# Self-edges taken out of layers 1 and 2 of a three-layer graph network: an edge list squeezed by VectorE during layer 0, and 197 steps a layer instead of 208

## What is computed

```python
h = x @ enc_W + enc_b
for l in range(3):
    cat = concatenate([h[src], h[dst], edge_features])            # 64 + 64 + 16
    m = relu(cat @ msg_W1[l] + msg_b1[l]) @ msg_W2[l] + msg_b2[l]
    agg = segment_sum(m, dst)
    h = gru_cell(agg, h, ...)
y = relu(h @ ro_W1 + ro_b1) @ ro_W2 + ro_b2
out = layernorm(x + y)
```

## Time and profile before

| | |
|---|---|
| timed runs, median of 3 | 6154.56 us |
| profiled execution: its own time (span) | 9775.6 us |
| gathers in it | 4830, of 0.955 us mean (4767 of them) |
| busy: GpSimd / VectorE / TensorE / ScalarE | 4639.2 / 3532.6 / 2880.1 / 346.4 us |
| TensorE granted clock | 0.571 mean |

### The profile page before, as it was taken

The page is one execution under the profiler, slowest core; times in us unless marked ns, Lnnn a source line. Parts: engine busy times, 40 slices in busy tenths (PEclk is TensorE's granted clock), DMA queues, the critical chain, the costliest instruction groups (busy, mean ns, idle before and its releaser), DMA issues.

```text
span 9775.6 us, 72182 instructions
## 1 busy us (share of the span) xinstructions
PE 2880.1 (29%) x7290; PEld 1610.2 (16%) x7290; DVE 3532.6 (36%) x4656; ACT 346.4 (4%) x542; POOL 4639.2 (47%) x4865
## 2 busy tenths in 40 slices
PE   3323322322322332222222222223232222322223
PEld 2111111111111221111111111112111111111112
DVE  2333333333333433333333333333333334333334
ACT  0000000000000000000000000000000000000001
POOL 5444444444444454444444444445454445545543
PEclk6555555555555555555555555555555555555555
DMA  3111111111111111111111111111111111111111
GB/s 87 31 31 30 30 30 30 28 31 30 31 30 30 30 28 30 30 30 30 30 30 29 30 30 27 30 31 30 30 31 31 30 30 34 31 31 31 31 30 25
DMA packets 351443, 308.63 MB, mean 32 GB/s; under 512 B 149364, under 2 KB 237518, under 8 KB 350568
## 3 DMA queue, kind: packets, MB, share of 16 engines
q0 software_dynamic: 155328, 159.79, 8.6%
q1 hardware_dynamic: 118271, 110.17, 4.0%
q10 hardware_dynamic: 77328, 33.96, 1.4%
HBM read 280.52 MB, written 22.83 MB: 31 GB/s over the span
## 4 chain that ended last, share of the span: by engine, by line
SPq 57%; issue 38%; DVE 2%; PE 1%; another core or an unknown queue 1%; DMA 0%; ACT 0%; POOL 0%; DVEq 0%; ACTq 0%; POOLq 0%
SPq L473 46%; SPq L469 6%; SPq L642 2%; SPq L633 1%; SPq L527 1%; DVE work_ps L1493 1%; SPq L630 1%; DVE folds L1528 0%; DVE p_src L1490 0%; PE bank L838 0%; DMA p_src<-p_tab 0%; PE work_ps L949 0%; PE bank L962 0%; SPq L662 0%
## 5 line engine op out<-in xcount | busy, mean ns | idle before, releaser
L798 POOL DMA_INDIRECT p_src<-p_tab,idx_all x4767 | 4551.1, 955 | 4916.8 <-DVE work_ps L1493 3467.4
L962 PE MATMUL bank<-hot,folds 128*128 128x96 f32 x2496 | 660.1, 413 | 4012.9 <-issue 2053.0
L1490 DVE TENSOR_TENSOR p_src<-work_ps,p_src 128x512 f32<-128x512 f32 x624 | 427.6, 685 | 3374.9 <-DMA p_src<-p_tab 2912.1
L962 PEld LDWEIGHTS bank<-hot,folds 128*128 128x128 f32 x2496 | 532.1, 296 | 4278.5 <-issue 2198.0
L949 PE MATMUL work_ps<-w_edges,msg 128*128 128x512 f32 x1248 | 1120.0, 997 | 21.4 <-DMA windows_sb<-q_tab 21.4
L1523 DVE SCALAR_TENSOR_TENSOR work_ps<-work_ps,rel 128x1024 f32<-128x1024 f32 x624 | 768.8, 1232 | 21.5
L1493 DVE TENSOR_TENSOR work_ps<-p_src,bank 128x1024 f32<-128x1024 f32 x624 | 767.0, 1229 | 21.4
L1528 DVE TENSOR_REDUCE folds<-work_ps 128x256 f32<-128x1024 f32 x624 | 758.4, 1215 | 0.0
L959 PE MATMUL bank<-hot,counts 128*34 128x96 bf16 x416 | 68.9, 261 | 2248.6 <-issue 1278.6
L1538 DVE TENSOR_TENSOR sums<-bank,sums 128x96 f32 x624 | 158.1, 253 | 872.6 <-remote 699.5
L959 PEld LDWEIGHTS bank<-hot,counts 128*34 128x34 bf16 x416 | 27.1, 108 | 2368.2 <-issue 1359.8
(11 more groups left out here) (167 smaller groups left out, 1800.9 us busy)
## 6 DMA issues: line engine op xcount, KB each, us to landing
p_src<-p_tab ACTq DMA_DIRECT2D x9792, 0.2 KB
p_src<-p_tab SPq DMA_DIRECT2D x9792, 0.2 KB
p_src<-p_tab,idx_all POOLq DMA_INDIRECT x4830
msg<-in_edge_k SPq DMA_DIRECT2D x156, 256.0 KB
pick<-rel_tab SPq DMA_DIRECT2D x312, 96.0 KB
windows_sb<-q_tab ACTq DMA_DIRECT2D x312, 24.0 KB
windows_sb<-q_tab SPq DMA_DIRECT2D x312, 24.0 KB
pick<-q_tab ACTq DMA_DIRECT2D x312, 24.0 KB
```

The costliest lines, as they stand in the source:

```text
L798: pool.indirect_dma_start(out=p_src[r][0:rows, t, :], out_offset=None, in_=p_tab[l][0:NODES, :], in_offset=bass.IndirectOffsetOnAxis(ap=id ...
L962: last = nc.tensor.matmul(fold_ps, folds[:, b, :], hot_all[n % 2][:, s * BLOCKS + b, 1:WINDOW + 1], start=(b == 0), stop=(b == BLOCKS - 1))
L1490: nc.vector.tensor_tensor(rows, edge_ps[k % 2], rows, ALU.add).then_inc(with_edge, 1)
```

## The change

Layer 0 is computed as before, over the whole list. Beside it the kernel makes a second edge list without the self-edges, and layers 1 and 2 use it: 197 steps (`PACKS`), each made from 1,080 edges of the original list, of which at most 1,024 are left. Group inputs of these layers come from tables in HBM that the kernel writes itself (`pack_edges`, `pack_rel_tab`, `pack_src`). The message of the self-edges (now one sum per node) is added per chunk. The parts:

- **Gathers.** `gathers_of`: a layer before has 208 x 8 - 51 - 3 = 1,610. Layers 1 and 2 now have 197 x 8 - 48 = 1,528 each. Layer 0 keeps 1,610.
- **Squeezing** (`press_step`, in groups 1 to 44 of layer 0). Two batches (100 and 97 packs, one pack per partition). Per batch 16 steps of preparation (`prepare`), then 18 planes (positions, sources, 16 edge features), a group each: 7 predicated copies over up to 1,095 elements (`shift`) and one reordering copy. SyncE loads and stores a plane each group.
- **Back into SBUF.** 8 pieces of up to 25 packs (`piece_load`): four transfers each, 128 x 25 runs of 4 words; `make_masks` makes new masks.
- **Loops.** In layer 0 `select_loops` (four VectorE instructions a group, one more input for SyncE), two small matmuls a step and one more add in `keep` give each node the features of its self-edges. In layers 1 and 2 each chunk has a matmul, an activation and an add more, and one ScalarE copy less.
- **Start.** New checks of the list (some 30 VectorE instructions over up to 2,160 elements); TensorE's two matmuls for the ranges stand behind the encoder, where they stood within it.

In the diff, in order: constants, `gathers_of`, SyncE in group g of layer 0, `piece_load`, VectorE's squeezing and `select_loops`, VectorE in a chunk of layers 1 and 2, and the start of TensorE's program.

```diff
+PACK = 1080
+PACK_SINGLES = 48
+BATCHES = ((0, 100), (100, PACKS - 100))
+PREP_GROUPS = 4
+PASS_LOW = (0, 0, 0, 0, 170, 368, 814)
+STEPS_OF = (STEPS, PACKS, PACKS)
...
+        def gathers_of(l, m):
+            return LAST_TILES if l == 0 and m == STEPS - 1 else EDGE_TILES - has_singles(l, m)
...
+                            if batch is not None and at >= PREP_GROUPS:
+                                pack_store(batch, at)
+                            batch, at = job(g - 1)
+                            if batch is not None and (at > PREP_GROUPS or (batch, at) == (1, 0)):
+                                pack_load(batch, at)
+                        for q in range(PIECES_ALL):
+                            if piece_loaded_at(q) == (l, g):
+                                piece_load(q)
...
+            def piece_load(q):
+                first, end = packs_of(q)
+                sp.wait_ge(packed_whole, 16 * (2 if end <= BATCHES[0][1] else 4))
+                sp.wait_ge(joined, end)
...
+                for b in range(BLOCKS):
+                    half = slice(b * RUN, (b + 1) * RUN)
+                    sp.dma_start(idx_all[:, first:end, half].bitcast(I32),
+                                 pack_src[first:end, b * RUN * 128:(b + 1) * RUN * 128].rearrange("u (r g) -> r u g", g=RUN)).then_inc(pack_idx_in, 16)
...
+            def shift(what, k, count):
+                low, high, by = PASS_LOW[k], PASS_HIGH[k], 1 << k
+                squeeze(nc.vector.copy_predicated(what[0:count, low:high], moves[k][0:count], what[0:count, low + by:high + by]))
...
+            def press_plane(batch, at, part):
...
+                if part < 2:
+                    shift(what, 2 * part, count)
+                    shift(what, 2 * part + 1, count)
+                elif part == 2:
+                    for k in range(4, SHIFTS):
+                        shift(what, k, count)
...
+            def select_loops(n):
...
+                nc.vector.tensor_tensor(edge_major[n % 2], edge_major[n % 2],
+                                        loop_runs[:].unsqueeze(2).to_broadcast([128, GROUP * BLOCKS, EDGE_DIM, RUN]), ALU.mult).then_inc(loop_steps, 1)
+                dve.wait_ge(loop_steps, 2 * n + 2)
+                nc.vector.tensor_reduce(loop_sel[n % 2], edge_major[n % 2], AX.X, ALU.add).then_inc(looped, 1)
...
+                if j == 0 and l:
+                    dve.wait_ge(loop_act, nth_loop(l, c) + 1)
+                    dve.wait_ge(kept, last_of(l, c) + 1)
+                    nc.vector.tensor_tensor(chunk_sum[0:HID, 0:w], zr[0:HID, 0:w], sums[0:HID, at + 1:at + 1 + w], ALU.add).then_inc(loop_added, 1)
...
-                if u == RANGES_AFTER:
...
-                    pe.wait_ge(apart_done, 1)
...
+            pe.wait_ge(vw_sb, LAYERS)
+            pe.wait_ge(reduced, 1)
...
+            pe.wait_ge(apart_done, 1)
```

More of the change, by code:

```diff
@@ L449, in nth_late, with where, group_of, begun @@
             return ((l - 1) * EARLY + m) * LATE_HOTS + q * LATE_BLOCKS + b
+        def where(k):
+            l = sum(k >= first for first in FIRST_STEP[1:])
+            return l, k - FIRST_STEP[l]
+        def group_of(l, m):
+            return FIRST_GROUP[l] + m // GROUP
+        def begun(n):
+            l = sum(n >= first for first in FIRST_GROUP[1:])
+            return FIRST_STEP[l] + min(GROUP * (n - FIRST_GROUP[l]), STEPS_OF[l])
+        def job(group):
+            batch, at = divmod(group - FIRST_JOB, BATCH_GROUPS)
+            return (batch, at) if 0 <= batch < len(BATCHES) else (None, None)
@@ L749, in _ @@
             for m in range(PRE):
-                for t in range(gathers_of(m)):
+                for t in range(gathers_of(0, m)):
                     pool.indirect_dma_start(
@@ L795, in _ @@
                             all_stored(pool, l, FAST_CHUNKS)
-                        for t in range(gathers_of(m)):
-                            rows = LAST_ROWS if m == STEPS - 1 and t == LAST_TILES - 1 else 128
+                        for t in range(gathers_of(l, m)):
+                            rows = LAST_ROWS if l == 0 and m == STEPS - 1 and t == LAST_TILES - 1 else 128
                             pool.indirect_dma_start(
@@ new lines, in _ @@
+            measured_by(last)
+            for i, (_, bound) in enumerate(MOST + LEAST):
+                last = nc.vector.tensor_scalar(measured[:, :, i], measured[:, :, i], float(bound), None, ALU.is_gt if i < len(MOST) else ALU.is_lt)
+            measured_by(last)
+            measured_by(nc.vector.tensor_reduce(pair_flags[0:PAIRED, 4:5], measured.rearrange("p j i -> p (j i)"), AX.X, ALU.add))
+            measured_by(nc.vector.tensor_scalar(far[:], row_f[:], 2.0 * PACK_RATE, -PACK_SLACK, ALU.mult, ALU.add))
@@ new lines, in _ @@
+            measured_by(nc.vector.tensor_scalar(pair_flags[:, 1:2], pair_flags[:, 1:2], 0.0, None, ALU.is_lt))
+            for j in range(2):
+                measured_by(nc.vector.tensor_tensor(apart[0:PAIRED], apart[0:PAIRED], measured[:, j, 0:1], ALU.add))
+            measured_by(nc.vector.tensor_tensor(apart[0:1], apart[0:1], measured[0:1, 0, 1:2], ALU.add))
+            measured_by(nc.vector.tensor_reduce(near[:], pair_flags[:], AX.X, ALU.add))
+            nc.vector.tensor_tensor(apart[:], apart[:], near[:], ALU.add).then_inc(apart_done, 1)
@@ new lines, in press_step, with make_masks @@
+            def press_step(m):
+                batch, at = job(m // GROUP)
+                if batch is None:
+                    return
+                if at < PREP_GROUPS:
+                    prepare(batch, at * GROUP + m % GROUP)
+                else:
+                    press_plane(batch, at, m % GROUP)
+            def make_masks(q):
+                first, end = packs_of(q)
+                count = (end - first) * BLOCKS
+                runs = pieces_i[q % 2][:, 0:end - first].rearrange("p u (b g) -> p (u b) g", g=RUN)
+                here = slice(first * BLOCKS, end * BLOCKS)
+                lead_edge = runs[:, :, 0:1].to_broadcast([128, count, RUN])
+                dve.wait_ge(piece_in[q % 2], 16 * BLOCKS * (q // 2 + 1))
+                nc.vector.tensor_copy(rel_first[:].rearrange("p u b -> p (u b)")[:, here], runs[:, :, 0])
+                nc.vector.tensor_tensor(masks[:, here, 0, :], runs, lead_edge, ALU.is_equal)
+                nc.vector.scalar_tensor_tensor(masks[:, here, 1, :], runs, -1.0, lead_edge, ALU.add, ALU.is_equal).then_inc(remasked, 1)
+                dve.wait_ge(remasked, q + 1)
@@ L1473, in landed @@
             def landed(k):
-                return 16 * sum(gathers_of(j % STEPS) for j in range(k % ROW_SLOTS, k + 1, ROW_SLOTS) if j >= PRE)
+                return 16 * sum(gathers_of(*where(j)) for j in range(k % ROW_SLOTS, k + 1, ROW_SLOTS) if j >= PRE)
             def edge_sums(k):
```

549 lines of the change are left out of this document (454 added, 95 removed).

## The result

| | us | beside the kernel before |
|---|---|---|
| before | 6155.32 (6151.95 to 6156.73, 4 runs) | |
| forecast | 6040 (5965 to 6210) | faster |
| after | 6451.16 (6447.2 to 6460.33, 4 runs) | 1.0483, 95% interval 1.0469 to 1.0498: slower |
| after, 100 rows in batch 2 (a run below) | 6087.86 (6085.66 to 6088.72, 4 runs) | 0.9891, interval 0.9874 to 0.9907: 1.1% shorter, clear of noise, but the same by a margin of 2% |

The account below looks back on a forecast made before the run. The prediction took GpSimd's gathers, 1.25 us each, as the bound: 6154.6 - 205 (gathers removed) + 80 (gathers held up by VectorE) + 8 (start) = 6,038, say 6040 us, with VectorE's and SyncE's added work at 0; range 5,965 to 6,210.

Parts of the forecast that it names:

- What bounds the kernel: Timed kernel: GpSimd gathers nearly all the time, 4,830 gathers at 1.25 us each; profiled execution bound by SyncE's single rows.
- Removed, -205 us: Layers 1 and 2: 164 fewer gathers at 1.25 us each, -205 us.
- Added: SyncE in layer 0 ... 0, hidden by that slack: SyncE's queue, layer 0: three more transfers a group, 1.4 us, cost 0 because SyncE has slack.
- slack: SyncE in layer 0: a group's rows, address loads and transfers take 25 us of 39.
- pieces of the list: Loads back into SBUF, seven in layer 0: 22 to 42 us each, cost 0, up to 40 us each without slack.
- VectorE's time, 0: Layer 0: VectorE's added work makes 8.6 us a step, 9.3 of 9.7 with waits, hidden by gathers: 0.
- Rival 2: Predicated copies take two passes an element, 2.3 us each, so VectorE becomes the bound: 6,177 us, chance 0.10.
- Gathers held up, +80 us: Gathers wait for VectorE's port: planes' copies 55 us, preparation 16, loops 5, chunks 4; +80 us, bounds 25 and 350.
- Rivals 1 and 3: 1: predicated copies don't hold gathers, 5,983 us, chance 0.14. 3: port held through whole gathers too, 6,307 us, chance 0.06.
- Start, +8 us: Range matmuls follow the encoder, so GpSimd restarts some 2 us after 95.1 and first step comes later: +8 us, 2 to 20.
- Rival 4: SyncE has no slack if a row takes 0.46 us, not 0.26: +230 us, 6,268 us, chance 0.13; decides from about 0.39.
- profile after: Profile of the changed kernel: again a span set by SyncE, near 9,550 us, with 4,666 gathers.

Follow-up runs that it names:

- rows100_3: The changed kernel with the second batch's loads, stores and squeezing over 100 rows instead of 97: 6087.86 us, 0.9891 of the kernel before.
- short100_2: rows100_3's kernel with the planes' predicated copies cut to 16 elements, lists of layers 1 and 2 not squeezed: 6083.13 us, 0.9885 of the kernel before.
- few100: Changed kernel, 100 rows in second batch, 28 of 64 single rows a group on each of SyncE and ScalarE, other 36 by plain transfers: 6086.16 us, 0.989.
- load100_4: The changed kernel with the second batch's loads of 100 rows and stores still of 97: 6333.55 us, 1.0289 of the kernel before.

## Why the forecast was wrong, step by step

- **What bounds the kernel: right, as far as it can be worked out.** The gathers of layers 1 and 2 follow each other without a wait in rows100_3 (9.77 us a step). 4,830 x 1.26, with 42.6 us ahead of the first gather and 30 behind the last (as in rows100_3), are 6,158 against 6,155 measured: the kernel before has next to no time besides gathers. The sum leaves out the 13.6 us that GpSimd idles before 95.1 us, and 1.26 us is good to some 0.3%, so it is exact to 10 or 20 us, and no trace of the kernel before from the timed kind confirms it. 1.26 us is a better figure than my 1.25, which left 60 us for other things. What I said of the profiled execution was off: it ran at its chip's own pace, and all timings of the kernel before on chips of that kind are as long.
- **Removed, -205 us: right.** 164 x 1.26 = 207; layers 1 and 2 run at 9.8 us a step even with 97 rows in the second batch, against 9.7 forecast.
- **"Added: SyncE in layer 0 ... 0, hidden by that slack": this step failed, by 363 us.** I counted what it takes to issue three more transfers (1.4 us) and never asked how long a plane's store and load themselves take, nor that an issue can wait behind them. Both transfers were in the diff (`BATCHES`, 97 rows), and no run had shown their price. A store of 20 us and a load of 17.5 behind it in one queue are longer than what hides them: SyncE is blocked 17 to 19 us a group, VectorE waits for both, and GpSimd's lead of seven steps runs out. Undoing only this gives 6,088.
- The **slack** was mis-sized too. A group's rows with their addresses take 25 us (the forecast had that for a whole group) and the rest 9 to 20 more: in the first batch of rows100_3 SyncE starts its rows every 34 to 35 and 45 to 50 us in turn, 40.4 at the mean (41.1 over groups 6 to 43), against 39 forecast for the gathers and some 41 that they take there. So there was no slack to hide anything longer. The pieces of the list are cheaper than feared: 12.4 us of issue for one of the first batch, not 22 to 42.
- **VectorE's time, 0: right** in rows100_3. It is busy 587 of 700 us there, 8.6 us of 10.2 a step; I had 8.6. From one copy of 1,095 elements to the next it is 1.4 us, not 1.29. Rival 2 (two passes, 2.3 us) is out. Its limit of "about 1.1 ns an element" did not follow from my numbers: 0.4 us of room a step are 0.26 ns an element more than the 1.04 taken, so 1.3.
- **Gathers held up, +80 us: the mechanism right, the size low.** 4,603 x (979 - 955 ns) = 110 us in rows100_3, 83 of them by the copies (979 - 961 ns, from short100_2; forecast 55). A place of rows100_3:

```profile
666.26 0.95 POOL L1071 DMA_INDIRECT p_src<-p_tab,idx_all  x1 [0.30 <-issue]
666.49 2.81 DVE L1847 COPY_PREDICATED pool_sb<-dst_i,pool_sb 100x1095 f32<-100x1095 uint8 x2
667.51 1.14 POOL L1071 DMA_INDIRECT p_src<-p_tab,idx_all  x1 [0.30 <-issue]
```

  The gather that had begun 0.23 us before neither waits nor holds the copies (2.81 us for two, their usual time). The one that begins 1.02 us into the first copy lasts 0.19 us longer. At its start 0.38 us of that copy were left, so it waited for the copy's end from a moment some 0.19 us after its own start, near the 0.13 us that I had worked out. The Trainium skill ("SBUF — State Buffer", section "SBUF: two separate sides") has an exclusive lock for the whole instruction; by that rule the copies would have waited too, and the trace does not agree. Rivals 1 and 3 are out. In the time itself the 110 us do not show on their own: short100_2 takes the copies' 83 us away and is 5 us faster, since SyncE's chain is as long.
- **Start, +8 us: wrong, 0 or a few us less.** The first `edge_sums` is at 117.16 us in rows100_3 and at 117.05 before. GpSimd idles 4.5 us there instead of 13.6 and goes on at 90.1 us instead of 95.1.
- **Rival 4** had the right queue but the wrong cause: not the price of a row, but one transfer that blocks the queue. A row costs 0.31 us (25 us less four address loads of 1.24, over 64), between the 0.26 taken and the 0.39 from which rival 4 was to decide. Its 6,268 was still 183 us short, and the range left even that out. That the result lies on rival 4's side is luck as far as the cause goes.
- With the failed step mended the sum is 6155 - 205 + 0 + 110 = 6,060 and rows100_3 measures 6,088. The 28 us left are not assigned, and the sum is no finer than the 10 or 20 us said above. The change of layers (5.1 and 9.6 us from one gather's start to the next, near 2,192 and 2,216 us) may hold half; that is read, not tested.
- The expected **profile after** was wrong: it was not drawn out, since its chip was of the timed kind.

## What to carry to other kernels

For every transfer that a change adds, ask what its outermost count divides into before asking what its issue costs: 97 rows moved on one DMA engine, 100 on several, and padding by three rows was worth 363 us of 6,451. Only 97, 100 and 101 rows were tried. A transfer that is short enough to hide must also not stand ahead of something in its queue; the issue of the next one waited 17 to 19 us for it. And when two chains are of equal length, cutting one shows nothing in the time: short100_2 and few100 each removed a real cost and gained 5 and 2 us.

## What the hardware showed that was not expected

- One program takes 6,155 us on some chips and about 9,800 on others, within 0.7% from run to run on one chip. The ranking changes with it: the changed kernel is 4.8% slower on one kind and 1.8% faster on the other (0.9822, 0.9796 to 0.9847). A profile must come from the kind of chip that is timed.
- The issue of a hardware-queue transfer can block for nearly as long as the transfer ahead of it runs: 17.44 us behind 776 packets of 512 bytes on one engine, which ran 19.7 us, and 0.68 us when they are spread (rows100_3). It is the one ahead that counts: in load100_4 the load behind is spread itself and still takes 18.94 us to issue.
- A predicated copy over 32-bit elements with a mask of bytes takes 1.37 us for 1,095 elements and 0.40 for 210 (means in rows100_3), that is 0.16 us + 1.11 ns an element, and a gather that starts in it waits for its end.
